# A four-layer graph network on one core: the destination sort, the edge rows and the sums of layer 1 rearranged

## The reference

```python
h = relu(layernorm(x)); x = x + L0(h, edge_index, edge_attr_32, ...)      # sum, max, mean of 32 edge features by source, then an MLP
h = relu(layernorm(x)); x = x + L1(h, edge_index, W, att_src, att_dst, bias)
   # logits = leaky_relu(a_src[src] + a_dst[dst]) for 8 heads (self loops added);
   # alpha = softmax of the logits over the edges of one dst; out = mean over heads of segment_sum(h[src] W * alpha, dst)
h = relu(layernorm(x)); x = x + L2(h, edge_attr_64, ...)
   # m = silu([edge, h[src], h[dst]] @ W1_msg + b1) @ W2_msg + b2; segment mean of m by dst; update MLP with silu
h = relu(layernorm(x)); x = x + L3(h, edge_index, edge_weight, edge_weight_n2, ...)
   # Wh = h W + b; cosine of Wh[row], Wh[col]; its weighted Wh[col] summed by row
```

## Time and profile before

| | us |
|---|---|
| median of three runs | 3962.55 |
| lowest and highest of the runs | 3942.38, 3967.39 |
| span of the profiled execution | 4718.9 |
| POOL busy in it | 2450.6 (52%) |
| DVE busy in it | 1840.9 (39%) |
| PE busy in it | 1124.4 (24%) |
| ACT busy in it | 244.1 (5%) |

### The profile page before, as it was taken

One profiled execution on the slowest core, in us unless ns is written; L12 is line 12 of the kernel. 1 busy time (PEld: TensorE's weight loads), 2 busy tenths in 40 slices (PEclk: granted clock), 3 DMA queues, 4 the chain that ended last, 5 costly groups with the idle time before them and its releaser, 6 DMA issues. The chain is left out here.

```text
span 4718.9 us, 22418 instructions
## 1 busy us (share of the span) xinstructions
PE 1124.4 (24%) x5316; PEld 921.6 (20%) x5317; DVE 1840.9 (39%) x5098; ACT 244.1 (5%) x433; POOL 2450.6 (52%) x2340
## 2 busy tenths in 40 slices
PE   1200001012000002311138778423435423000001
PEld 0200001002000001201136667313324322000000
DVE  7732222865321007000013431134545541476665
ACT  0000000001000001000000001111112101000000
POOL 0577774022776656677740000355758722677773
PEclk9999999996555555655555555555555555555555
DMA  0111110111556650222221110212222201122121
GB/s 9 18 15 15 13 17 7 64 68 25 58 56 57 54 50 17 50 55 48 57 76 51 55 29 1 64 45 79 82 69 88 68 23 17 33 48 49 36 48 42
DMA packets 177464, 207.12 MB, mean 44 GB/s; under 512 B 123566, under 2 KB 134287, under 8 KB 170968
## 3 DMA queue, kind: packets, MB, share of 16 engines
q0 software_dynamic: 74336, 102.76, 11.2%
q1 hardware_dynamic: 46552, 88.76, 5.7%
q10 hardware_dynamic: 56480, 14.64, 4.9%
HBM read 128.05 MB, written 77.96 MB: 44 GB/s over the span
## 5 line engine op out<-in xcount | busy, mean ns | idle before, releaser
L535 POOL DMA_INDIRECT l2g_rows<-tab,l2g_ring_idx x440 | 516.5, 1174 | 210.6 <-issue 135.0
L574 POOL DMA_INDIRECT l0g_rows<-in_rec_s,ents x440 | 476.1, 1082 | 288.0 <-DVEq L420 149.3
L535 POOL DMA_INDIRECT l3g_rows<-tab,l3g_ring_idx x440 | 485.5, 1103 | 160.9 <-issue 137.6
L948 POOL DMA_INDIRECT ep_rows<-in_rec_d,ep_ring_idx x440 | 447.9, 1018 | 174.0 <-issue 131.0
L535 POOL DMA_INDIRECT l1g_rows<-tab,l1g_ring_idx x440 | 423.3, 962 | 177.0 <-issue 133.5
L1378 PE MATMUL l1a_pa<-l1a_g,l1a_wt 128*128 x1288 | 295.4, 406 | 249.2 <-issue 249.1
L1378 PEld LDWEIGHTS l1a_pa<-l1a_g,l1a_wt 128*128 128x128 f32 x1288 | 287.5, 327 | 283.3 <-issue 283.2
L1662 PE MATMUL l2g_pu<-l2g_wm,l2g_at 64*128 64x64 f32 x880 | 214.5, 424 | 456.3 <-ACT l2g_at L1680 299.2
L1615 POOL DMA_INDIRECT l2g_first<-tab,node0d x1 | 1.0, 1014 | 571.8 <-POOLq L154 571.8
L1662 PEld LDWEIGHTS l2g_pu<-l2g_wm,l2g_at 64*128 64x128 f32 x880 | 195.2, 325 | 496.9 <-ACT l2g_at L1680 308.3
L1403 DVE TENSOR_TENSOR acc<-acc,l1a_pa 128x455 f32 x92 | 53.7, 625 | 530.6 <-remote 330.3
(11 more groups left out here) (463 smaller groups left out, 2497.0 us busy)
## 6 DMA issues: line engine op xcount, KB each, us to landing
l1a_g<-g SPq DMA_DIRECT2D x46, 455.0 KB
rowsd<-ep_rows POOLq DMA_DIRECT2D x10, 1452.0 KB
l2g_u<-rowsd SPq DMA_DIRECT2D x10, 1452.0 KB
g<-l1g_rows ACTq DMA_DIRECT2D x10, 1430.0 KB
sums<-l0s_sums SPq DMA_DIRECT2D x10, 1408.0 KB, 4.8
sums<-l2g_sums SPq DMA_DIRECT2D x10, 1408.0 KB
sums<-l3g_sums SPq DMA_DIRECT2D x10, 1408.0 KB
l0g_rows<-in_rec_s,ents POOLq DMA_INDIRECT x440
```

What stands on the lines that cost most here:

```text
L535: nc.gpsimd.indirect_dma_start(out=ring.rows[:, s, j, :], out_offset=None, in_=table, in_offset=bass.IndirectOffsetOnAxis(ap=ring.idx[:, s ...
L574: nc.gpsimd.indirect_dma_start(out=rows[:, j, :], out_offset=None, in_=K.a["rec_s"], in_offset=bass.IndirectOffsetOnAxis(ap=K.by_src.ent[: ...
L948: nc.gpsimd.indirect_dma_start(out=ring.rows[:, s, j, :], out_offset=None, in_=K.a["rec_d"], in_offset=bass.IndirectOffsetOnAxis(ap=ring.i ...
```

## The change

1. `sort_destinations` takes the place of sorts "p" and "e": both destination orders lie side by side in one 128 x 1024 array, each DVE instruction twice as wide, eight transposes and two ACT copies at each exchange. It runs beside layer 0's gather; nothing is sorted in layer 1.
2. `EdgeTable`: the 64 edge features of all entries are read once (`edges_t`, 14.4 MB), projected by the first 64 rows of `W1_msg` on PE during the first sort and stored; the edge gathers read the projected rows. `layer2_gather` no longer projects.
3. `list_setup`: instead of 20 wide one-hots and 440 matmuls, nine groups of three matmuls (441 columns).
4. `layer0_sums`, `layer2_gather`, `layer3_gather`: ACT copies a block, features outermost, into PSUM with one extra column for the carried value, and masks into SBUF; one DVE scan runs over a whole block (1440, 2880 or 2925 numbers) where 32, 64 or 65 scans of 44 ran; ACT copies the sums back. The last block of layer 2 is cut into 22, 14 and 8 columns.
5. `early_edges`: 88 of the 440 edge gathers (two blocks of 44) move into `layer0_finish`, 22 ahead of the collect's 25 and 66 behind; `remaining_edges` gathers the other 352 in layer 1, each block's store issued ten gathers into the next.
6. `layer1_gather`: the ring belongs to the caller, ACT's stores are waited for only by those who read them, `layer1_items` runs with `act_ahead` (a meeting without ACT).
7. `layer1_sums`: 54 bodies of 12 items, 128 moving columns for each item instead of 65, three zeroing matmuls of 512 columns instead of two of 455, one DVE add of 12 x 65.
8. `layer1_tail` joins `layer1_finish`, the normalisation and `layer2_tables` in a pipeline over groups of tiles; `layer2_tail` does so for layer 2's finish and layer 3's table.

The diff, cut to the parts spoken of:

```diff
 def layer1_gather(K):
...
-                for s in range(RING):
-                    act.wait_ge(stored[s], NBLK // RING * 16)
-        sort_keys(K, "e", K.a["nodesd"], K.by_dst.key, alone=True)
-        edge_order(K)
-        layer1_items(K)
...
+            rounds(act, body)
+    layer1_items(K)
...
 def layer0_finish(K):
...
+        early_edges(K, 0, EARLY)
         collect(K, K.by_src, K.sums0, D // 2, res, True)
+        early_edges(K, EARLY, RING * TB - EARLY)
...
 def layer1_sums(K):
...
-                        for i in range(2):
-                            nc.tensor.matmul(pa[b][:, i * 512:i * 512 + SPAN], zero[:, 0:P], zero[:, 0:SPAN], start=True, stop=False)
+                        for i in range(0, IB, 4):
+                            nc.tensor.matmul(pa[b][:, i * P:(i + 4) * P], zero[:, 0:P], zero[:, :], start=True, stop=False)
                         for u in range(IB):
-                            nc.tensor.matmul(pa[b][:, bass.ds(places[u], D + 1)], wt[:, b, u].rearrange("p h s -> p (h s)"),
-                                                  g[:, b, bass.ds(slots[u], 1), :].rearrange("p o d -> p (o d)"), start=False, stop=False)
+                            nc.tensor.matmul(pa[b][:, bass.ds(places[u], P)], wt[:, b, u].rearrange("p h s -> p (h s)"),
+                                             g[:, b, bass.ds(slots[u], P)], start=False, stop=False)
...
-                    for i in range(2):
-                        sums = K.acc[:, bass.ds(w + 7 * i, 7), :].rearrange("p w d -> p (w d)")
-                        last = v.tensor_tensor(sums, sums, pa[b][:, i * 512:i * 512 + SPAN], ALU.add)
-                    last.then_inc(added, 1)
+                    sums = K.acc[:, bass.ds(w, IB), :]
+                    v.tensor_tensor(sums, sums, used[b], ALU.add).then_inc(added, 1)
...
+                    nc.scalar.copy(mix[:, :, 1:], ring.rows[:, s, c0:c0 + n, D:].rearrange("p j f -> p f j")).then_inc(spread, 1)
...
-                        for f in range(D):
-                            v.tensor_tensor_scan(r[:, s, :, D + f], kb[:, :], r[:, s, :, D + f], q[:, f:f + 1], ALU.mult, ALU.add)
...
+                    v.tensor_tensor_scan(flat(mix), keeps[:, 0:size], flat(mix), 0.0, ALU.mult, ALU.add)
```

More of the change, by code:

```diff
@@ L48 @@
 R2 = 128
-R3 = 66
+R3 = 2 * (D + 1)
+FLAT = TB + 1
+SETTLE = 10
+EARLY = TB // 2
+EB = 40
+NEB = J // EB
+UNITS = J // 8
+STAGES = 2
+LOADS = ((0, 1), (1, 3), (3, 6), (6, NEB))
+LAST = ((0, 22), (22, 14), (36, 8))
+GROUPS = [(w, min(4, NT - w)) for w in range(0, NT, 4)]
+NG = len(GROUPS)
 class Kern:
@@ L217, in sems, with sort_sources @@
         return [self.sem(n) for n in names]
-def sort_keys(K, name, nodes, key, first=False, pairs=False, alone=False):
+def sort_sources(K):
     nc = K.nc
     W = SORT_W
-    with Phase(K, "sort" + name) as ph:
+    with Phase(K, "sorts") as ph:
         raw = ph.sb("raw", [P, W], I32)
-        other = ph.sb("other", [P, 2, W], I32) if pairs else None
         X = [ph.sb("x0", [P, W]), ph.sb("x1", [P, W])]
@@ new lines, in turn_buffers, with turn_blocks @@
+def turn_buffers(X):
+    side = 0
+    for k in range(1, 17):
+        for b in range(k - 1, -1, -1):
+            if k >= 10 and b in (k - 1, 8):
+                yield X[side], X[1 - side]
+                side = 1 - side
+            side = 1 - side
+def turn_blocks(nc, pe, X, turn_ps, ident, ready, turned):
+    n = X[0].shape[1] // SORT_W
+    for m, (c, t) in enumerate(turn_buffers(X)):
+        pe.wait_ge(ready, m + 1)
+        for h in range(n):
+            for g in range(4):
+                at = h * SORT_W + g * P
+                last = nc.tensor.transpose(turn_ps[m % 2][h][:, g * P:(g + 1) * P], c[:, at:at + P], ident)
+        last.then_inc(turned, 1)
@@ new lines, in _ @@
+                for t, (w, n) in enumerate(groups):
+                    dve.wait_ge(fetched, t + 1)
+                    v.tensor_tensor(inside[:, t % 2, 0:n], rows[t % 2][:, 0:n, 0:J],
+                                    limit[:, w:w + n].unsqueeze(2).to_broadcast([P, n, J]), ALU.is_gt)
+                    v.tensor_copy(start[:, w:w + n], rows[t % 2][:, 0:n, J])
+                    v.drain().then_inc(counted, 1)
+                    v.tensor_reduce(count[:, w:w + n], inside[:, t % 2, 0:n], AX.X, ALU.add)
@@ L487, in _ @@
-                nc.tensor.matmul(hist[0:HI, 0:LO], zero[:, 0:HI], zero[:, :], start=False, stop=True).then_inc(p2, 1)
-                pe.wait_ge(dn, 2)
-                nc.tensor.matmul(basep[0:HI, 0:1], K.lower[:, :], run[:, LO - 1:LO], start=True, stop=True).then_inc(p2, 1)
+                for t, (w, n) in enumerate(groups):
+                    pe.wait_ge(hot, t + 1)
+                    if t >= 2:
+                        pe.wait_ge(counted, t - 1)
+                    for i in range(n):
+                        last = nc.tensor.matmul(rows[t % 2][:, i, 0:J + 1], held[:, (w + i) * P:(w + i + 1) * P], turned[:, :],
+                                                start=True, stop=True)
+                    last.then_inc(fetched, 1)
@@ L512, in block_cols, with gather_rounds, body @@
     return bass.ds((it * size + s) * TB, TB)
-def gather_rounds(nc, pool, ring, table, idx, freed, taken=None):
-    def body(it, first):
+def gather_rounds(nc, pool, ring, table, idx, freed, taken=None, last=None):
+    def body(it, first, ends=None):
         for s in range(ring.size):
@@ L534, in body @@
             for j in range(TB):
+                landed = ring.gathered[s]
+                if ends is not None and s == ring.size - 1:
+                    landed = [sem for (c, n), sem in zip(LAST, ends) if c <= j < c + n][0]
                 nc.gpsimd.indirect_dma_start(
@@ L942, in gather, with remaining_edges, _ @@
+            for s in range(RING):
+                if first + n == RING * TB:
+                    store_edges(K, nc, pool, slice(s * TB, (s + 1) * TB), s, TB * 16)
+def remaining_edges(K):
+    nc = K.nc
+    ring, stored = K.rows.ring, K.rows.stored
+    with Step(nc, meet=False) as block:
+        @block.gpsimd
+        def _(pool):
+            def gather(it, s, between=None):
                 nc.gpsimd.tensor_copy(ring.idx[:, s, :], K.by_dst.ent[:, block_cols(it, s)]).then_inc(ring.indexed, 1)
-                pool.wait_ge(ring.indexed, it * RING + s + 1)
@@ L1093, in _ @@
             def _(pe):
+                for s in range(RING):
+                    pe.wait_ge(K.l1.kept[s], NBLK // RING)
                 for r in range(2 * H):
@@ new lines, in layer1_tail, with wide_of @@
+        scaled, turned, moved, headed, kept, returned = ph.sems("scaled", "turned", "moved", "headed", "kept", "returned")
+        added, spread, rooted, normed, turned2, moved2 = ph.sems("added", "spread", "rooted", "normed", "turned2", "moved2")
+        second, tabled = ph.sems("second", "tabled")
+        stored = [ph.sem(f"stored{i}") for i in range(TABS)]
+        last = NT % 2 and len(PAIRS) - 1
+        def wide_of(u):
+            return D if u == last else P
+        with Step(nc) as block:
```

1671 lines of the change are left out of this document (1106 added, 565 removed).

## The result

The changed kernel takes 3301.77 us (3298.41 to 3303.47, four runs) against 3964.24; the ratio is 0.8343, with a 95% interval of 0.832 to 0.8365.

What follows compares the result with a forecast made beforehand. No engine bound the kernel throughout (POOL busiest, 52%); the bound changed from stage to stage. On stages rebuilt to 3927 us without stretches, terms summed to -466, taken from the 3962.55 us median: 3496, range 3340 to 3690.

Steps and rivals of the forecast that it cites:

- a body takes 5.7, 308 us: Layer 1's sums: if wider bodies bring the 2.4 GHz clock, a body takes 5.7 us, the stage 308, -103.
- part of the stage at the low clock: 340: Layer 1's sums: high clock likelier, but part of the stage at the low one, so 340 us, -70.
- the disturbance of POOL: Layer 2's gather: DVE passes over two SBUF operands lengthen POOL's DMAs, 1174 ns against 962; the whole 93 us go.
- 50 of disturbance: Layer 0's gather after the change: 550 us of pitch plus 50 us still lost to DVE's wide pairs.
- 28 us at worst: Layer 0's finish: the collect waits behind 22 early edge gathers, 22 x 1.25 = 28 us; stage +28.
- lie beside an MLP and tables: Layer 0's finish: the 66 later early gathers, 82 us, run beside about 85 us of other work.
- these end no wait that I can find: Layer 1: moving 110 us of edge gathers earlier shortens nothing, so the gain was costed at nothing.
- the forecast's own low-clock case: Rival for layer 1's sums: they stay at 1.2 GHz, +97 for -70, total 3663; chance 0.24.
- the block chain: Layer 2's gather: copies, flat scans, adds and pack per block take some 33 us, hidden under POOL's 55.
- rival 3: Layers 2 and 3: strided copies make the flat form slower than before, 4005; chance 0.05 with its mild form.
- I take this as the profiler's work: Whole kernel: the profile's 756 us over the median come from profiling, so the run was rebuilt without them.
- Rival 2: Stretches beside gathers are the chip's, not the profiler's, so the change removes more: about 3250; chance 0.10.

Runs made afterwards that it cites:

- experiments 3 and 11: Changed kernel with 65 moving columns in the sums' matmuls instead of 128: 3405.01 us; with 96, on a slower chip: 4176.67 us against 4059.47.
- the second profile: The kernel before, unedited, profiled again: 3934.94 us, span 3933.3 us.
- experiment 5: Changed kernel with 65 moving columns in the sums and all 440 edge gathers back in layer 1: 3392.9 us.
- experiment 9: Changed kernel, unedited, run several times on a slower chip: 4059.47 us against 4749.34 for the kernel before, ratio 0.8543.

## Why the prediction was wrong

The gain is 196 us larger than forecast. The stages of the table hold 166 of them; the other 30 lie between the profile and the median of the kernel before.

**The sums, -170 for -70: 100 us of the miss.** The failed step is the term "a body takes 5.7, 308 us" with "part of the stage at the low clock: 340". The mechanism (width brings the clock) was the one that experiments 3 and 11 show, though no row of the prediction had shown it. But bodies are 4.6 us apart, 24 instructions of 0.1225, which makes 251 us for 308: 57 us. Another 32 are that I averaged a two-way outcome into 340, a value that neither way has, and 10 that the sums before take 421 us and not 411. The range of the forecast had no case for "high clock throughout, and faster than estimated", 251 us.

**Layer 2, -177 for -138, and layer 0, -56 for -24: 71 us.** The failed step is the disturbance of POOL, read as 93 us in layer 2 from the mean of 1174 ns. In that profile DVE was itself stretched and its passes met fewer DMAs; the second profile has 562.6 us busy for 415.8 after, 147 us. The mechanism was right in half of it only. In the second profile 35 DMAs, each beside a wide pass, lose 77 us, but six DMAs of 11.7 us, each beside a run of scans at L1721, lose 64 us. The prediction put the whole on passes over two operands and left the scans out, though the first profile had three DMAs of 9.4 to 11.7 us beside L1721 too. So part of this gain is scans removed that I had not priced. The remaining 30 us of layer 2 are the last block and collect (49.8 us behind the last gather, now 20.0), where the forecast had 47 and 25. In layer 0 the gather's busy time fell by 64 us (498.6 to 434.8), more than the whole change of that stage, and 58 us of it are the forty one-hot passes (L454, L456), each beside a DMA of 2.1 to 2.7 us. There the 84 us that I had counted for before (62 in the row and "22 more") met the 83 of the second profile, while the "50 of disturbance" for after were 19: here the mechanism was right and the size was not.

**Layer 0's finish, +11 for +28, and the early edges.** Three errors in one step. "28 us at worst" was taken as the value though the 22 gathers had cover, and cost 3.7. The 66 that were to "lie beside an MLP and tables" cost 17. And "these end no wait that I can find" was wrong for the kernel after: I set 440 us against a chain of 606, which held the whole 137 of the tail, though the weights and the fetch behind the meeting (55 us) can't start until the edges are stored, and held 340 for the sums. With 127 + 251 + 83 the chain is 461, and the edges end with it. In the forecast's own low-clock case the claim would have been right (experiment 5).

**Layer 2's finish, -28 for -50.** The pipeline takes 111 us. The forecast had 60 us of chain behind 31 of collect, and the chain is 80. A window of it has PE busy 73.19 of 114 us, at the low clock; that this is the cause was not tried.

```profile
2541.00:2655.00 114.00, 73.19 (x232) 45.51 (x232) 38.88 (x115) 34.84 (x53) 26.16 (x27) 0.50 0.27 32
```

**Right within 6 us:** layer 1's gather with the meeting behind it, layer 1's tail (223 and 140, forecast 223 and 137), layer 3, and the block chain, 30 us for 33. The flat scan takes 6.16 us (6.1 forecast); rival 3 is out, since the copy that turns a block takes 4.86 us, above the 3.3 of the forecast but far from 12.7:

```profile
2080.33 4.86 ACT L2204 COPY l2g_mix<-l2g_rows 128x2816 f32<-128x2816 f32 x1 [21.12 <-DMA l2g_rows<-tab,l2g_ring_idx]
```

**The reading of the first profile.** "I take this as the profiler's work" was most likely wrong in cause (experiment 9) and right in use, and that was luck: the times of the result came from chips without the stretches. The rebuilt stages (3927) met the second profile (3933), six of ten within 5 us; layer 1's gather with its gap was 40 too long (652 for 612), layer 2's 39 too short (713 for 752), the sums 10 too short, so the sum fits better than its parts. Rival 2 said that the stretches are the chip's: on one chip of this record they are there in every execution. Its price (3250) assumed them in the measured time; where they are, the ratio is 0.8543 and the gain 690 us, for 0.8343 and 662 where they aren't.

## What to carry to other kernels

When one engine issues gathers from end to end, look in the trace for DMAs that are held beside passes and scans over SBUF, and move those passes' data to PSUM: in layers 2 and 3 the gain wasn't the time of the passes but that no DMA is held. A narrow matmul that keeps the engine fully busy at the low clock can be made faster by columns that are thrown away, when nothing else ends at the same time; test the width, 65, 96 and 128, before estimating. And where two chains run towards one meeting, price an edit of one only together with the edit of the other.
